# Attention output products scaled and added to the residual by VectorE, in a decoder layer on one core

## Chip, cores and metric

One core of a Trainium2 chip runs the whole layer in one launch. The metric is the device time of an execution in microseconds (us), as the median of several runs.

## What is computed

The reference is one decoder layer on x of 128 sequences x 128 tokens x 256 features, fp32. Cut to what matters here:

```python
x = x + attn(layernorm(x))                    # 16 heads of 16, self-attention
x = x + xattn(layernorm(x), ctx, ctx, mask)   # 16 heads of 16, keys and values from ctx
x = x + ffn(layernorm(x))                     # ternary weights, GELU, layernorm inside

def attn(x):
    ...
    out = einsum('bhqk,bhkd->bhqd', softmax(scores), V).transpose(0, 2, 1, 3).reshape(B, S, D)
    return out @ Wo.T + bo
```

The change touches the last line of each attention: the output product `out @ Wo.T`, and its addition to `x + bo`.

## The kernel before

**Jobs and slots.** The sequences are taken in 32 groups of 4 (G = 4, so 512 tokens). Each group is a self-attention job and, some slots later, a cross-attention job: 64 jobs in a fixed order, six self jobs first (LEAD = 6), then cross and self in turn, then the last six cross jobs. They run through a software pipeline. In slot n, job n+4 is loaded, n+3 has its moments taken, n+2 is normalised (`s.norm`), n+1 is projected to queries and keys (`s.proj`), n has its scores and maxima taken and its values projected (`s.max`), n-1 its exponentials and weighted sums (`s.exp`), and n-2 its output product and residual (`s.out`). Slots run from -3 to 65. Jobs alternate between two sets of buffers and semaphores, `even` and `odd`; in each slot `a` is the chain of jobs n and n-2, `b` that of n-1 and n+1. After the attention slots comes the feed-forward stage, whose order the change leaves alone.

**Order.** Nothing is scheduled automatically. Each engine's queue in a slot is the list of calls at the end of `pool_slot`, `act_slot`, `dve_slot` and `pe_slot` (SyncE's is in `sp_slot`); engines wait for one another by semaphores.

**Precision.** Products are fp16 in three parts (high x high, low x high, high x low). ScalarE makes the high part by a copy to fp16, GpSimd the low part by subtracting it (`low`, L735). Weights carry a factor WS = 8, so the output product is divided by 8 when it leaves its banks.

**Banks.** TensorE's results lie in four tensors of two banks each: `score_bank` (scores, L1049, with mask matmuls L1030), `exp_bank` (shifted scores, L1067; for cross jobs also the masked values' products, L1167), `out_bank` (weighted sums, L1082) and `product_bank`. The last is shared by three users in turn within a slot: the query and key tiles (L1106), the output products (`products`, L1113, two calls for batches 0, 1 and 2, 3) and the value products (`values`, also L1113). The values may overwrite the banks only when the output products have been read.

**Around the change.** The output product leaves in two steps. ScalarE's `products_out` (L844 to 852) waits for the products (`op_mm`) and for `xs_lo`, as GpSimd must have read the normalised values from `xn` before `xn` is written; it copies both banks, scaled by 1/WS, to `xn` and raises `op_out`. GpSimd's `residual` (L749 to 752) then adds the block `xb` (input plus output bias, made by `biased` at L764 two slots earlier) and raises `y_ready`, on which SyncE's `store` waits. TensorE's `values` waits for `op_out`:

```python
if s.out:
    pe.wait_ge(a.op_out, s.out.k + 1)
```

**VectorE in a slot.** Eight score maxima (`maximum`, L906, a reduction of 128x1024 out of `score_bank`), four query and key tiles (L912), four quarter outputs (`outputs`: a transposition L940, for cross jobs an addition L947, a reciprocal L951 and a product L955), two transpositions of the attention output (`turn_att`, L961), then the negated maxima (`negate`, L967 or L969) and the moments (L980 to L986). The order of its second half is `maximum(5)`, `outputs(b, s.exp, 1)`, `turn_att(b, s.exp, 0)`, `maximum(6)`, `outputs(b, s.exp, 2)`, `maximum(7)`, `negate()`, `moments()`. TensorE's is `products(2, 3)`, `shifted(6)`, `scores(6)`, `weighted(2)`, `values(0, 1)`, `scores(7)`, `shifted(7)`, `values(2, 3)`, `turn_maxima()` (L1148, waits for `negate`), `masked_values()` (L1167, waits for ScalarE's `values_out`, L857), `weighted(3)`. ScalarE's is `exps(5)` (L811), `products_out()`, `exps(6)`, `exps(7)`, `values_out`.

Of the kernel before, what the change touches and what calls it, by code (L numbers as in the profile page):

```python
# [12 lines left out]
ALU = mybir.AluOpType  # L13
# [499 lines left out]
class Chain:  # L513
# [3 lines left out]
    def __init__(self, name, sb, sem):  # L517
# [49 lines left out]
        self.op_mm = sem(n + "_op_mm")  # L567
        self.op_out = sem(n + "_op_out")
        self.y_ready = sem(n + "_y_ready")


def attention(nc, program, ins, sh, x1_dram, x2_dram, prep):
# [19 lines left out]
    with ExitStack() as stack:  # L592
# [137 lines left out]
        def pool_slot(pool, s, bias_done=None):  # L730
# [17 lines left out]

            def residual():  # L749
                if s.out:  # L750
                    pool.wait_ge(a.op_out, s.out.k + 1)
                    nc.gpsimd.tensor_tensor(xn[:, :, :], xn[:, :, :], a.xb[:, s.out.k % 2], ALU.add).then_inc(a.y_ready, 1)

            def biased():
# [26 lines left out]
            low_norm()  # L781
            residual()
            biased()
# [4 lines left out]
        def act_slot(s):  # L788
# [3 lines left out]
            def await_store():  # L792
                if s.past:
                    act.wait_ge(stored_by(s.past), 16 * (s.past.g + 1))
# [48 lines left out]

            def products_out():  # L844
                if s.out:
                    act.wait_ge(a.op_mm, s.out.k + 1)
                    if s.norm:
                        act.wait_ge(a.xs_lo, s.norm.k + 1)
                    else:
                        await_store()  # L850
                    act.activation(xn[:, :, :].rearrange("p b d -> p (b d)"), pbank[:, :, :].rearrange("p a d -> p (a d)"),
                                   ACT.Copy, scale=1.0 / WS).then_inc(a.op_out, 1)

            def values_out(n):
# [31 lines left out]
            exps(5)  # L886
            products_out()
            exps(6)
# [8 lines left out]
        def dve_slot(s):  # L897
# [59 lines left out]
            def turn_att(ch, job, kt):  # L957
                if job:

                    dve.wait_ge(ch.ao_ready, 4 * job.k + 2 * kt + 2)  # L960
                    dve.transpose(attT[:, kt], att[:, kt]).then_inc(ch.aT_ready, 1)  # L961

            def negate():
                if s.max:
# [43 lines left out]
            outputs(b, s.exp, 1)  # L1008
            turn_att(b, s.exp, 0)
            maximum(6)  # L1010
            outputs(b, s.exp, 2)
# [10 lines left out]
        def pe_slot(s):  # L1022
# [106 lines left out]
            def values(*batches):  # L1129
                if s.max is None:  # L1130
                    return
                for g in batches:
                    if g == 0:
                        if s.out:
                            pe.wait_ge(a.op_out, s.out.k + 1)
                        elif s.proj:
                            pe.wait_ge(b.qk_lo, 4 * s.proj.k + 4)
# [371 lines left out]
```

## Time and profile before

| | |
|---|---|
| median of 3 runs | 2367.21 us (2365.73 to 2368.36) |
| profiled execution, its own time | 2370.91 us |
| its span, first to last instruction | 2369.1 us |
| mean granted TensorE clock | 0.984 of full speed |
| two neighbouring slots in the middle | 25.17 and 26.85 us |

The profile is of one execution. Times in timelines are from the start of the span. The attention slots end at about 1796 us, the rest is the feed-forward stage. PE is TensorE's matmuls, PEld its weight loads, DVE VectorE, ACT ScalarE, POOL GpSimd, SP SyncE; L906 is line 906 of the kernel. In a timeline a bracket names the idle time of the engine ahead of the row and what ended it; a row without one began with no idle time worth naming. Matmul rows overlap by some hundredths of a us, since matmuls are pipelined.

### The profile page before, as it was taken

To read this page: it belongs to the slowest core of one execution; us is meant where nothing else is said; L and a number is where in the kernel's file an instruction comes from. 1 tells how busy PE (TensorE), PEld (TensorE's weight loads), DVE (VectorE), ACT (ScalarE), POOL (GpSimd) and SP (SyncE) were. 2 spreads that over 40 slices of the span, in tenths; PEclk is the share of its full clock that TensorE was granted. 3 is DMA by queue.
4 is the path that set the end of the run, shared out by engine and by line. 5 is a ranking of instruction groups with operands and counts; after the bars stand their busy time and mean duration, and the time that the engine had idled before them with its cause. 6 is when DMAs were issued, how large, how long until landed. Compare 5 with 4: busy or idle time off the path is not lost.

```text
span 2369.1 us, 70234 instructions
## 1 busy us (share of the span) xinstructions
PE 2183.7 (92%) x29033; PEld 1449.4 (61%) x29033; DVE 1933.5 (82%) x3903; ACT 1596.8 (67%) x2354; POOL 1044.4 (44%) x849
## 2 busy tenths in 40 slices
PE   4689999999999999999999999999967999999999
PEld 2356656656665666566566656655544777777776
DVE  5788888888888888888888888887745788887887
ACT  3377666667666666666666666665535878778786
POOL 2144443454444344444434444454224554555543
PEclk9799999999999999999999999999978999999999
DMA  4567666676666667666666766676422333333332
GB/s 129 117 151 175 156 144 155 145 158 157 157 153 152 155 140 159 157 160 153 154 150 143 153 161 157 159 173 144 89 59 54 84 103 80 97 89 83 103 81 63
DMA packets 472860, 311.01 MB, mean 131 GB/s; under 512 B 288144, under 2 KB 423184, under 8 KB 472592
## 3 DMA queue, kind: packets, MB, share of 16 engines
q1 hardware_dynamic: 469488, 306.80, 55.0%
q8 instruction: 205, 3.36, 0.6%
q10 hardware_dynamic: 3104, 0.34, 0.1%
q14 instruction: 63, 0.52, 0.1%
HBM read 71.65 MB, written 50.33 MB: 51 GB/s over the span
## 4 chain that ended last, share of the span: by engine, by line
PE 65%; DVE 18%; ACT 7%; issue 7%; SPq 1%; DMA 1%; POOL 1%; DVEq 0%; ACTq 0%; POOLq 0%
PE product_bank L1106 14%; PE ybk L1434 9%; PE hbk L1458 9%; PE out_bank L1082 7%; PE tbk L1448 5%; ACT prob L811 4%; PE product_bank L1113 4%; PE score_bank L1030 4%; DVE out_bank L940 4%; PE score_bank L1049 3%; DVE odd_mx L906 3%; PE exp_bank L1067 3%; PE exp_bank L1030 3%; PE exp_bank L1167 3%; DVE att L955 2%
## 5 line engine op out<-in xcount | busy, mean ns | idle before, releaser
L811 ACT ACTIVATE prob<-exp_bank 128x1024 f32<-128x1024 f32 x512 | 523.1, 1022 | 254.6 <-PE exp_bank L1067 246.6
L735 POOL TENSOR_TENSOR xs<-xn,xs 128x1024 f16<-128x1024 f32 x64 | 136.3, 2130 | 638.8 <-ACT xs L835 638.8
L906 DVE TENSOR_REDUCE even_mx<-score_bank 128x8 f32<-128x1024 f32 x256 | 310.5, 1213 | 97.4 <-PE score_bank L1049 97.4
L906 DVE TENSOR_REDUCE odd_mx<-score_bank 128x8 f32<-128x1024 f32 x256 | 310.2, 1212 | 81.0 <-PE score_bank L1049 81.0
L801 ACT ACTIVATE qk<-product_bank,bcol 128x512 f16<-128x512 f32 x256 | 175.9, 687 | 232.0 <-PE product_bank L1106 228.7
L1458 PE MATMUL hbk<-wfcT,ffn_xhl 128*128 128x512 f16 x1024 | 264.5, 382 | 6.3 <-ACT hid L1355 3.4
L1418 DVE SCALAR_TENSOR_TENSOR ghl<-tbk,lnwc,ghl 128x512 f16<-128x512 f32 x256 | 188.0, 735 | 100.3 <-ACT ghl L1349 100.3
L1434 PE MATMUL ybk<-wpT,ghl 128*128 128x256 f16 x2048 | 260.5, 273 | 0.8 <-DVE ffn_y L1403 0.7
L1434 PEld LDWEIGHTS ybk<-wpT,ghl 128*128 128x128 f16 x2048 | 197.8, 98 | 66.1 <-DVE ghl L1418 0.9
L1349 ACT ACTIVATE ghl<-tbk,lnwc 128x512 f16<-128x512 f32 x256 | 174.1, 681 | 68.1 <-PE tbk L1448 68.1
L940 DVE STREAM_TRANSPOSE out_bank<-out_bank 128x512 f32<-128x512 f32 x256 | 183.5, 717 | 24.8 <-PE out_bank L1082 24.7
L912 DVE SCALAR_TENSOR_TENSOR qk<-product_bank,bcol,qk 128x512 f16<-128x512 f32 x256 | 184.2, 740 | 22.4 <-ACT qk L801 22.4
L1030 PE MATMUL exp_bank<-maskBT,pick 64*128 64x512 bf16 x1024 | 156.5, 385 | 45.3 <-ACT prob L811 27.7
L1113 PE MATMUL product_bank<-WT,ahl 128*128 128x256 f16 x1536 | 192.9, 276 | 4.8 <-POOL ahl L735 4.8
L735 POOL TENSOR_TENSOR ahl<-attT,ahl 128x512 f16<-128x512 f32 x128 | 148.6, 1161 | 100.6 <-ACT ahl L816 100.6
L1379 DVE BATCH_NORM_STATS2 hstats<-hid 128x6 f32<-128x512 f32 x256 | 174.1, 680 | 16.5 <-ACT hid L1355 16.4
L1355 ACT ACTIVATE hid<-hbk 128x512 f32<-128x512 f32 x256 | 152.4, 596 | 51.0 <-PE hbk L1458 44.0
L1106 PE MATMUL product_bank<-odd_xhl,WT 128*128 128x512 f16 x732 | 176.0, 384 | 7.6 <-DVE qk L912 5.6
L1113 PEld LDWEIGHTS product_bank<-WT,ahl 128*128 128x128 f16 x1536 | 141.4, 99 | 34.3 <-POOL ahl L735 5.1
L1030 PE MATMUL score_bank<-maskB,pick 64*128 64x512 bf16 x1024 | 154.7, 381 | 6.3 <-DVE even_mx L906 5.6
L1448 PE MATMUL tbk<-ident,hid 128*128 128x128 f32 x1024 | 154.4, 274 | 0.7 <-ACT hid L1355 0.7
L1458 PEld LDWEIGHTS hbk<-wfcT,ffn_xhl 128*128 128x128 f16 x1024 | 98.2, 98 | 75.1 <-ACT hid L1355 5.2
(174 smaller groups left out, 4401.3 us busy)
## 6 DMA issues: line engine op xcount, KB each, us to landing
even_stk<-qk SPq DMA_DIRECT2D x384, 128.0 KB, 2.7
odd_stk<-qk SPq DMA_DIRECT2D x384, 128.0 KB, 2.8
x_scratch<-xn SPq DMA_DIRECT2D x64, 512.0 KB, 4.8
ctx_in<-in_ctx SPq DMA_DIRECT2D x32, 512.0 KB, 4.6
ffn_src<-x_scratch SPq DMA_DIRECT2D x32, 512.0 KB, 3.8
out<-ffn_y SPq DMA_DIRECT2D x32, 512.0 KB, 3.7
odd_src<-in_x SPq DMA_DIRECT2D x29, 512.0 KB, 5.4
even_src<-x_scratch SPq DMA_DIRECT2D x29, 512.0 KB, 5.5
```

The source lines that it names most:

```text
L735: nc.gpsimd.tensor_tensor(out, src, hi, ALU.subtract).then_inc(lo_ready, 1)
L811: act.activation(prob[:, p % 3], ebank[:, :, :], ACT.Exp, scale=EXP_SCALE).then_inc(b.exp_done, 1)
L906: dve.tensor_reduce(a.mx[:, g * H:(g + 1) * H].rearrange("p (r e j) -> p r e j", r=2, e=2)[:, :, eight], sbank[:, :, :].rearrange("p r (j ...
L912: dve.scalar_tensor_tensor(qk[:, 3 * (n // 2), n % 2], pbank[:, n % 2], sh.bcol[:, 2 * s.proj.which + n // 2, n % 2:n % 2 + 1], qk[:, 1 + ...
L940: dve.transpose(obank[:, 1], obank[:, 0]).then_inc(ch.o_turned, 1)
L1030: pe.matmul(bank[:, r].rearrange("p (b s) -> p b s", b=G), sh.pick[rows, h], mask[rows, h].unsqueeze(1).broadcast_to([HALF, G, S]), start= ...
L1106: last = pe.matmul(pbank[:, n % 2].rearrange("p (b s) -> p b s", b=G), sh.WT[:, (s.proj.wq, s.proj.wk)[n // 2], wp, kt, n % 2 * P:(n % 2 + ...
L1113: last = pe.matmul(pbank[:, g // 2, g % 2 * D:(g % 2 + 1) * D], stationary(part, g, kt), sh.WT[:, w, wp, kt, :], start=(k == 0 and kt == 0 ...
L1418: dve.scalar_tensor_tensor(ghl[:, LO, s], tbk[:, TURN_BANK[s]], sh.lnwc[:, s:s + 1], ghl[:, HI, s], ALU.mult, ALU.subtract).then_inc(glo_r ...
L1434: last = pe.matmul(ybk[:, b], ghl[:, part, t, b * S:(b + 1) * S], sh.wpT[:, t], start=(t == 0 and part == HI and b % 2 == 0), stop=(t == F ...
L1448: last = pe.transpose(tbk[:, TURN_BANK[s], b * S:(b + 1) * S], hid[:, 1 - half, b, s * P:(s + 1) * P], sh.ident[:, :])
L1458: last = pe.matmul(hbk[:, s % 2], xhl[:, half, part, s // 2, kt], sh.wfcT[:, kt, s % 2 * HF:(s % 2 + 1) * HF], start=(part == HI and kt == ...
```

## The change

ScalarE's `products_out` and GpSimd's `residual` go, and with them the semaphore `op_out`. VectorE gets a `residual` that reads both banks, multiplies by 1/WS, adds `xb` and writes `xn`, in one operation; it stands between `turn_att(b, s.exp, 0)` and `maximum(6)`. TensorE's value products wait for `y_ready`, which this operation raises.

```diff
@@ pool_slot
-            def residual():
-                if s.out:
-                    pool.wait_ge(a.op_out, s.out.k + 1)
-                    nc.gpsimd.tensor_tensor(xn[:, :, :], xn[:, :, :], a.xb[:, s.out.k % 2], ALU.add).then_inc(a.y_ready, 1)
...
             low_norm()
-            residual()
             biased()
@@ act_slot
-            def products_out():
-                if s.out:
-                    act.wait_ge(a.op_mm, s.out.k + 1)
-                    if s.norm:
-                        act.wait_ge(a.xs_lo, s.norm.k + 1)
-                    else:
-                        await_store()
-                    act.activation(xn[:, :, :].rearrange("p b d -> p (b d)"), pbank[:, :, :].rearrange("p a d -> p (a d)"),
-                                   ACT.Copy, scale=1.0 / WS).then_inc(a.op_out, 1)
...
             exps(5)
-            products_out()
             exps(6)
@@ dve_slot
+            def residual():
+                if s.out:
+                    dve.wait_ge(a.op_mm, s.out.k + 1)
+                    dve.wait_ge(a.xb_ready, s.out.k + 1)
+                    if s.norm:
+                        dve.wait_ge(a.xs_lo, s.norm.k + 1)
+                    elif s.past:
+                        dve.wait_ge(stored_by(s.past), 16 * (s.past.g + 1))
+                    dve.scalar_tensor_tensor(xn[:, :, :].rearrange("p b d -> p (b d)"), pbank[:, :, :].rearrange("p a d -> p (a d)"), 1.0 / WS,
+                                             a.xb[:, s.out.k % 2].rearrange("p b d -> p (b d)"), ALU.mult, ALU.add).then_inc(a.y_ready, 1)
...
             turn_att(b, s.exp, 0)
+            residual()
             maximum(6)
@@ pe_slot, values
                         if s.out:
-                            pe.wait_ge(a.op_out, s.out.k + 1)
+                            pe.wait_ge(a.y_ready, s.out.k + 1)
```

**VectorE's queue**, second half of a slot whose newest job is a self job (odd chain) and whose exponentials are of a cross job. Rows are line, operation, output<-inputs, the semaphores waited for. Before:

```order
L955 TENSOR_TENSOR att<-out_bank,rec 128x16x16 [waits even_rec_ready]
L961 STREAM_TRANSPOSE attT<-att 128x512 [waits even_ao_ready]
L906 TENSOR_REDUCE odd_mx<-score_bank 128x2x4 [waits odd_s_mm]
L940 STREAM_TRANSPOSE out_bank<-out_bank 128x512 [waits even_pv_done,even_ao_ready]
L947 TENSOR_TENSOR out_bank<-out_bank,ue 128x16x17 [waits even_o_turned]
```

And with the change:

```order
L937 TENSOR_TENSOR att<-out_bank,rec 128x16x16 [waits even_rec_ready]
L943 STREAM_TRANSPOSE attT<-att 128x512 [waits even_ao_ready]
L953 SCALAR_TENSOR_TENSOR xn<-product_bank,odd_xb 128x1024 [waits odd_xs_lo,odd_xb_ready,odd_op_mm]
L888 TENSOR_REDUCE odd_mx<-score_bank 128x2x4 [waits odd_s_mm]
L922 STREAM_TRANSPOSE out_bank<-out_bank 128x512 [waits even_pv_done,even_ao_ready]
```

One operation has come in ahead of maximum 6, with three waits; the order is otherwise the same.

**TensorE's queue** at the value products of an early slot. Before:

```order
L1082 MATMUL out_bank<-prob,odd_vals 32x128 [waits odd_o_turned,odd_exp_done]
L1082 MATMUL out_bank<-prob,odd_vals 32x128 x15
L1113 MATMUL product_bank<-WT,even_xhl 128x256 [waits even_op_out]
L1113 MATMUL product_bank<-WT,even_xhl 128x256 x11
L1049 MATMUL score_bank<-even_stk 128x128 [waits even_max_done]
```

And with the change:

```order
L1076 MATMUL out_bank<-prob,odd_vals 32x128 [waits odd_o_turned,odd_exp_done]
L1076 MATMUL out_bank<-prob,odd_vals 32x128 x15
L1107 MATMUL product_bank<-WT,even_xhl 128x256 [waits even_y_ready]
L1107 MATMUL product_bank<-WT,even_xhl 128x256 x11
L1043 MATMUL score_bank<-even_stk 128x128 [waits even_max_done]
```

Nothing has moved on TensorE; one wait has another semaphore, raised by another engine.

## Rows read from the trace of the kernel before

**Rows 1.** The page: busy time by engine, and the chain that ended last.

```profile
PE 2183.7 (92%) x29033; PEld 1449.4 (61%) x29033; DVE 1933.5 (82%) x3903; ACT 1596.8 (67%) x2354; POOL 1044.4 (44%) x849
...
PE 65%; DVE 18%; ACT 7%; issue 7%; SPq 1%; DMA 1%; POOL 1%; DVEq 0%; ACTq 0%; POOLq 0%
```

**Rows 2.** Lines L851 and L752: durations min/median/max in ns; waiters in us and times.

```profile
L851 ACT ACTIVATE xn<-product_bank x64: 1024/1026/1030, 139.8 to 1794.6; 128x1024 f32<-128x1024 f32 x64
...
  PEld product_bank L1113: 3.2, 5
  PE product_bank L1113: 1.9, 4
...
L752 POOL TENSOR_TENSOR xn<-xn,even_xb x32: 2353/2356/2373, 140.9 to 1780.5; 128x1024 f32<-128x1024 f32 x32
```

**Rows 3.** Two neighbouring slots: length, then busy us of PE, PEld, DVE, ACT, POOL.

```profile
814.38:839.55 25.17, 23.59 (x367) 15.05 (x366) 21.83 (x35) 17.15 (x23) 8.28 (x8) 1.00 0.58 134
839.55:866.40 26.85, 25.71 (x413) 16.58 (x414) 23.09 (x46) 18.35 (x26) 15.00 (x13) 1.00 0.75 172
```

**Rows 4.** VectorE by line, whole span: count | busy us, mean ns | idle before.

```profile
L906 DVE TENSOR_REDUCE even_mx<-score_bank 128x8 f32<-128x1024 f32 x256 | 310.5, 1213 | 97.4 <-PE score_bank L1049 97.4
...
L912 DVE SCALAR_TENSOR_TENSOR qk<-product_bank,bcol,qk 128x512 f16<-128x512 f32 x256 | 184.2, 740 | 22.4 <-ACT qk L801 22.4
...
L1403 DVE SCALAR_TENSOR_TENSOR ffn_y<-ybk,hrstd,ffn_y 128x256 f32<-128x256 f32 x128 | 52.8, 474 | 1.1 <-PE ybk L1434 1.1
```

**Rows 5.** Timeline, second half of a C slot: start us, us, engine, line.

```profile
803.37 2.13 POOL L735 TENSOR_TENSOR xs<-xn,xs 128x1024 f16<-128x1024 f32 x1 [8.69 <-ACT xs L835]
...
803.48 1.49 PE L1113 MATMUL product_bank<-WT,ahl 128*128 128x256 f16 x12
...
806.65 1.19 DVE L906 TENSOR_REDUCE even_mx<-score_bank 128x8 f32<-128x1024 f32 x1
...
806.89 1.48 PE L1113 MATMUL product_bank<-WT,ctx_hl 128*128 128x256 f16 x12
...
807.76 0.71 DVE L940 STREAM_TRANSPOSE out_bank<-out_bank 128x512 f32<-128x512 f32 x1
...
809.46 1.02 ACT L811 ACTIVATE prob<-exp_bank 128x1024 f32<-128x1024 f32 x1 [1.94 <-PE exp_bank L1067]
...
811.52 1.99 PE L1167 MATMUL exp_bank<-even_vals,maskcT 128*32 128x256 f32 x32 [0.22 <-ACT even_vals L857]
```

**Rows 6.** Timeline, second half of the S slot that follows.

```profile
833.79 1.19 DVE L906 TENSOR_REDUCE odd_mx<-score_bank 128x8 f32<-128x1024 f32 x1
...
833.98 1.48 PE L1113 MATMUL product_bank<-WT,odd_xhl 128*128 128x256 f16 x12
...
838.01 0.23 DVE L969 TENSOR_TENSOR odd_negm<-odd_mx,mshift 128x64 f16<-128x64 f32 x1
...
838.29 0.33 PE L1148 MATMUL score_bank<-ident,odd_negm 128*16 128x128 f16 x3 [0.42 <-DVE odd_negm L969]
```

**Rows 7.** Timeline of VectorE, start of slot 4.

```profile
171.42 0.75 DVE L912 SCALAR_TENSOR_TENSOR qk<-product_bank,bcol,qk 128x512 f16<-128x512 f32 x1 [0.64 <-ACT qk L801]
```

**Rows 8.** Timeline, a slot of the last six (cross jobs alone).

```profile
1615.76 1.18 DVE L906 TENSOR_REDUCE odd_mx<-score_bank 128x8 f32<-128x1024 f32 x1
...
1616.38 0.83 PE L1113 MATMUL product_bank<-WT,ctx_hl 128*128 128x256 f16 x6
```

**Rows 9.** Timeline, end of attention, slot 65.

```profile
1794.63 1.02 ACT L851 ACTIVATE xn<-product_bank 128x1024 f32<-128x1024 f32 x1 [6.62 <-PE product_bank L1113]
...
1795.73 2.34 POOL L752 TENSOR_TENSOR xn<-xn,odd_xb 128x1024 f32<-128x1024 f32 x1 [6.49 <-ACT xn L851]
```

**Rows 10.** Timeline of TensorE, two waits for VectorE at about 1630 and 1661.

```profile
1629.60 1.47 PE L1106 MATMUL product_bank<-ctx_hl,WT 128*128 128x512 f16 x6 [1.84 <-DVE qk L912]
...
1661.28 2.25 PE L1106 MATMUL product_bank<-ctx_hl,WT 128*128 128x512 f16 x6 [1.83 <-DVE qk L912]
```

**Rows 11.** The stretch after the second: columns as in rows 3, then clock, DMA, GB/s.

```profile
1661.00:1666.00 5.00, 4.72 (x32) 1.97 (x33) 2.77 (x5) 2.29 (x3) 1.16 (x1) 0.66 0.47 89
```

More of the change, by code:

```diff
@@ L567, in __init__ @@
         self.op_mm = sem(n + "_op_mm")
-        self.op_out = sem(n + "_op_out")
         self.y_ready = sem(n + "_y_ready")
```

## Prediction, made blind

> **What bounds the kernel now.** I read the page first, then the chain that ended last, then the timelines of two neighbouring slots, since shares of busy time say little about which wait ends last. The page [rows 1] shows TensorE busy for 92% of the span, VectorE 82%, ScalarE 67% and GpSimd 44%. So the change takes work from the two engines with room and gives it to one that has little. The chain of waits [rows 1] runs 65% over TensorE, 18% over VectorE, 7% over ScalarE and 1% over GpSimd. The reader should see that GpSimd's additions are practically never on it.
>
> The two removed instructions are 64 ScalarE copies of 1.03 us and 64 GpSimd additions of 2.36 us [rows 2]. Who waited for them? Nobody for the additions. The copies held TensorE 5 times in its weight load, 3.2 us in all, and 4 times in its matmul, 1.9 us in all [rows 2]; the store of the block of rows stands on SyncE's queue behind the transfer of the maxima, which comes later in the slot anyway. About 5 us is therefore all that the whole removal can give back inside the slots.
>
> A slot is one pass of the pipeline; the two kinds in the middle take 25.17 and 26.85 us [rows 3]. From its middle on, VectorE alternates between score maxima and the quarter outputs, and TensorE alternates between scores, shifted scores, weighted sums and products. Call a slot **C** when its newest job is cross-attention (slots 6, 8 to 58) and **S** when it is self-attention with a cross job in the exponentials (7, 9 to 57). These are 27 and 26 slots; 2 to 5 are self alone, 59 to 63 cross alone, 64 and 65 the tail.
>
> **The new instruction.** A VectorE operation on 128x1024, fp32 from the banks, fp32 from SBUF and to SBUF, does not occur before. The same operation on 128x256 takes 474 ns, one on 128x512 (fp16 out) 740 ns, and a reduction that reads 128x1024 out of a bank 1213 ns [rows 4]. From 256 to 512 elements the price is 266 ns, 1.04 ns per element. So 1024 elements cost 740 + 512 x 1.04 = 1273 ns. Ends: 1.21 us (the reduction, the nearest in size) and 1.48 us (twice the 512 one, its fixed part paid twice). I take 1.27 us. On VectorE the following instruction starts some 0.08 us before the end of the one in front (the maximum of 806.65 lasts 1.19 us, its successor starts at 807.76 [rows 5]), so the queue is moved by 1.27 - 0.08 = **1.19 us**.
>
> **S slots.** The operation stands behind the transposition of the outputs and ahead of maximum 6. What it waits for is there by then, as the C slot below shows with its numbers. It starts where maximum 6 started, at 833.79 [rows 6]. From there to the negation at 838.01 no row of VectorE carries idle time, and TensorE starts the transposition of the maxima behind it at 838.29 [rows 6]; the last weighted sum and the next slot's projections stand behind that. This is the place where VectorE is the bound: +1.19 us. TensorE's own new wait costs no more: the value products now wait for y_ready, which comes at 833.79 + 1.27 + 0.06 = 835.12 where they started at 833.98 [rows 6], 1.14 us, in parallel. 26 x 1.19 = **30.9 us**.
>
> **C slots.** Here VectorE starts maximum 6 at 806.65 [rows 5]. The products (12 matmuls from 803.48, 1.49 us) are ready at 804.97 and GpSimd's low part at 803.37 + 2.13 = 805.50 [rows 5], so again only VectorE's queue sets the start. y_ready comes at 806.65 + 1.27 + 0.06 = 807.98; the value products started at 806.89 [rows 5]. TensorE waits 1.09 us. Queued behind them on TensorE are scores 7 and shifted scores 7, for which ScalarE waits with its last exponential at 809.46; then come ScalarE's values, the masked products at 811.52 [rows 5] and the next slot. VectorE's negation, also 1.19 us later, stays just hidden beside this. 27 x 1.09 = **29.4 us**.
>
> **The rest.** In slots 2 to 5 VectorE is the bound as in S: 4 x 1.19, of which one slot gives back 0.64 us, since VectorE waits there for ScalarE, and that for the stacking transfers [rows 7]: 4.1 us. In 59 to 63 TensorE has more work: maximum 6 starts at 1615.76, so y_ready is at 1617.09 where the products started at 1616.38 [rows 8]: 5 x 0.71 = 3.6 us. In slot 65 the copy starts at 1794.63 and the addition ends at 1795.73 + 2.34 = 1798.07 [rows 9]; the next stage's first variance stands behind it on GpSimd. The new operation would end at 1794.63 + 1.27 = 1795.90, 2.2 us sooner, but the aggregation of the means now stands behind it on VectorE, and the GELU, which has its own table load and matmuls ahead, takes over soon: I count -1 us. Removed ScalarE time otherwise comes at a point where it next waits for TensorE: nothing.
>
> Sum: 30.9 + 29.4 + 4.1 + 3.6 - 1.0 = **+67 us**. The profiled execution took 2370.9 us (span 2369.1), the median of the runs is 2367.2: 3.7 us lower. I set the forecast on the median: 2367.2 + 67 = 2434, and give **2435 us**.
>
> **Two rules weighed.** The rows first: VectorE without idle time in the second half of S, 82% over the span [rows 1, 6]. The Trainium skill, page Perfetto Trace Analysis, section Optimizing Scalar/DVE Operations, says that a saturated VectorE is a reason to hand work to ScalarE or even GpSimd; this change does the reverse. By that rule alone every slot would pay the full step, 64 x 1.19 = 76 us, against 67 by the rows.
> The other speaks for the change: GPSIMD Engine Reference, section Engine selection, sends elementwise additions to VectorE, as GpSimd needs about twice the time for two inputs. The trace agrees on the durations (2.36 against an expected 1.27 us [rows 2, 4]), but nobody waits for the 2.36.
>
> **The rivals.**
> - *The released engines were the bound* (the other side, faster). ScalarE waits for GpSimd's low parts ahead of each copy; without copy and wait its exponential 6 comes over 1 us sooner. For it: 9 waits of TensorE on the copy [rows 2] and the tail [rows 9]. If VectorE's added step hid in its idle time, 5.1 + 1.0 us come back: 2361 us. It decides if y_ready comes before TensorE asks for it, so if VectorE reached the place over 1 us sooner than it does. Against it: VectorE has no gap between the last quarter output and maximum 6 in either slot. Were every copy and addition in series on the path, as the rule on GpSimd would suggest, it would be 64 x (1.03 + 2.36 - 1.27) = 136 us less, 2231 us; that nobody waits for the additions [rows 2] denies it. Both together 0.03.
> - *Only VectorE's own bound counts*. In C slots TensorE's wait is absorbed by the ones it has further on (0.2 us before the masked products [rows 5], others after). Then the 29.4 us fall away: 2405 us. Against it: those waits are for ScalarE, whose work hangs on the same delayed matmuls. 0.07.
> - *The clock falls*. TensorE stands at 2.4 GHz nearly throughout, but from 1661 to 1666 the granted clock was 0.66 [rows 11], partly at 1.2 GHz: six matmuls took 2.25 us after a wait of 1.83, where they took 1.47 after one of 1.84 [rows 10]. The stretch lost 5 x 0.34 = 1.7 us. The new waits are near 1.1 us each, and each slot goes on as densely as before. If they did bring it in each C and S slot, it would be 53 x 1.7 = 90 us more: 2525 us. 0.05. The Trainium skill (TensorE: Matmul & The Clock Gate, Part 1) says that idleness sends the clock back to its lower level; by rows 10 a single wait of 1.8 us may or may not do it.
> - *Nothing measurable*, because both new waits are covered by something that I don't see: 0.02.
>
> **The numbers.** My forecast has 0.83. Its own bounds: with 1.21 us for the operation 58 slots give 3 to 4 us less; with 1.48 us, 12 us more. Two more waits on the instruction (three semaphores instead of one) are not priced by any row: between nothing and 0.1 us each, 12 us more. If a part of the C slots' wait is absorbed (half: 15 us less), it is about 2417. Range **2410 to 2460**; outside lie the 2405 case, the clock case and the fast ones, under 2 in 10. Within 0.2% is 4.7 us, about what a measurement of this kernel can tell from no change. Faster 0.03, same 0.02, slower 0.95.
>
> **What would show it.** VectorE has 64 operations of about 1.27 us from product_bank to xn, without a wait ahead of them in slots 2 to 63, and its busy time is 81 us higher; ScalarE's is 66 us lower, GpSimd's 151 us. TensorE has a new wait at the value products on VectorE, about 1.1 us and 58 times. C and S slots are each 1.1 to 1.2 us longer, a pair 54.3 instead of 52.0 us, and the stage behind attention keeps its length. I am wrong if the operation takes over 1.5 us, if slots grow by less than half of this while the wait is there (absorption), if the granted clock falls in the middle of attention, or if VectorE reaches the place with idle time ahead.

## The result, and the profile after

| | before | with the change |
|---|---|---|
| median of the runs | 2367.78 us (4 runs, 2365.73 to 2368.45) | 2435.15 us (4 runs, 2433.18 to 2435.99) |
| profiled execution, its own time | 2370.91 us | 2435.99 us |
| its span | 2369.1 us | 2434.2 us |

The ratio is 1.0279, with a 95% interval from 1.0264 to 1.0294: the change makes the kernel 2.8% slower, 67 us. The forecast was 2435 us.

The page of the changed kernel, the lines of [rows 1]:

```profile
PE 2190.0 (90%) x29033; PEld 1450.1 (60%) x29033; DVE 2004.9 (82%) x3967; ACT 1537.4 (63%) x2290; POOL 892.7 (37%) x785
...
PE 60%; DVE 22%; issue 9%; ACT 6%; DMA 1%; SPq 0%; POOL 0%; DVEq 0%; ACTq 0%; POOLq 0%
```

ScalarE has become 59 us less busy, GpSimd 152 us less, VectorE 71 us more. The 64 removed ScalarE copies lasted 66 us; the remaining ScalarE operations count some 6 us more than before. In the chain that ended last VectorE's share rose from 18% to 22% and TensorE's fell from 65% to 60%, while GpSimd's went from 1% to nothing. Over 200 us of work left two engines, and the kernel became longer: neither was what the slots waited for.

The new operation, by its line, with those who waited for it:

```profile
L953 DVE SCALAR_TENSOR_TENSOR xn<-product_bank,even_xb x32: 1183/1185/1186, 143.1 to 1848.4; 128x1024 f32<-128x1024 f32 x32
L953 DVE SCALAR_TENSOR_TENSOR xn<-product_bank,odd_xb x32: 1183/1184/1224, 167.3 to 1862.7; 128x1024 f32<-128x1024 f32 x32
its engine sat idle before it (us, times) until:
  PE product_bank L1107: 7.0, 1
who waited for it (us, times):
  PEld product_bank L1107: 75.4, 62
  PE product_bank L1107: 58.9, 62
```

It takes 1.18 us, a little less than foreseen, and VectorE stood idle ahead of it once, in the tail. TensorE's matmuls waited for it in each of the 62 slots that have value products, 58.9 us in all: 0.95 us each. ScalarE's copy had held them 4 times, 1.9 us in all [rows 2]. The weight load in front of the matmuls waits for the same event, so its own sum (75.4 us now, 3.2 us before) is not added to theirs.

Two neighbouring slots, each from the first projection matmul to the next slot's, S and then C. The columns are those of [rows 3]:

```profile
845.57:871.87 26.30, 23.66 (x367) 15.06 (x365) 22.95 (x36) 16.16 (x22) 6.00 (x8) 1.00 0.55 128
871.87:899.71 27.84, 25.77 (x415) 16.56 (x413) 24.07 (x48) 17.50 (x25) 12.54 (x11) 1.00 0.73 166
```

Against 25.17 and 26.85 us [rows 3] they are 1.13 and 0.99 us longer. TensorE does the same 23.7 and 25.8 us of work at the same full clock; the added time is idle time on it.

The timeline of a C slot, the place of [rows 5]:

```profile
835.82 0.42 DVE L937 TENSOR_TENSOR att<-out_bank,rec 128x256 f32<-128x256 f32 x1
...
836.27 0.71 DVE L943 STREAM_TRANSPOSE attT<-att 128x512 f32<-128x512 f32 x1
836.91 1.19 DVE L953 SCALAR_TENSOR_TENSOR xn<-product_bank,even_xb 128x1024 f32<-128x1024 f32 x1
838.02 1.21 DVE L888 TENSOR_REDUCE even_mx<-score_bank 128x8 f32<-128x1024 f32 x1
...
838.15 1.48 PE L1107 MATMUL product_bank<-WT,ctx_hl 128*128 128x256 f16 x12 [0.93 <-DVE xn L953]
...
840.72 1.02 ACT L804 ACTIVATE prob<-exp_bank 128x1024 f32<-128x1024 f32 x1 [4.10 <-PE exp_bank L1061]
...
841.78 0.28 DVE L960 SCALAR_TENSOR_TENSOR even_negm<-even_mx,mfloor,mshift 128x64 f16<-128x64 f32 x1
...
842.12 0.39 PE L1142 MATMUL score_bank<-ident,even_negm 128*16 128x128 f16 x4
```

And of an S slot, the place of [rows 6]:

```profile
865.05 1.19 DVE L953 SCALAR_TENSOR_TENSOR xn<-product_bank,odd_xb 128x1024 f32<-128x1024 f32 x1
866.16 1.21 DVE L888 TENSOR_REDUCE odd_mx<-score_bank 128x8 f32<-128x1024 f32 x1
...
870.40 0.23 DVE L962 TENSOR_TENSOR odd_negm<-odd_mx,mshift 128x64 f16<-128x64 f32 x1
```

VectorE goes from the transposition (836.27) to the residual to the maximum without a gap, each of the two starting some hundredths before the one in front has ended (836.91 + 1.19 = 838.10, next start 838.02). From the residual's start to the maximum's is 1.11 us, the step by which the queue is moved. ScalarE shows where the freed time went: its last exponential has 4.10 us of idle time ahead, where 1.94 us stood before [rows 5]. TensorE turns the maxima at 842.12 without idle time ahead, though VectorE's negation has moved too: beside TensorE's own wait of 0.93 us that delay stays hidden, as the prediction had it.

The negations of the maxima stand at the same place in each slot, and so cut the span into comparable stretches. From the rows of their two lines, self and cross:

```profile
L962 DVE TENSOR_TENSOR odd_negm<-odd_mx,mshift x29: 225/226/226, 123.7 to 1628.8; 128x64 f16<-128x64 f32 x29
...
L960 DVE SCALAR_TENSOR_TENSOR odd_negm<-odd_mx,mfloor,mshift x3: 283/286/286, 1684.7 to 1814.6; 128x64 f16<-128x64 f32 x3
```

Before, the same rows ran from 120.8 to 1566.1 us (slots 1 and 57) and to 1744.4 us (slot 63).

| stretch | before | after | difference | forecast |
|---|---|---|---|---|
| start to negation of slot 1 | 120.8 | 123.7 | +2.9 | 0 |
| slot 1 to slot 57 | 1445.3 | 1505.1 | +59.8 | 4.1 + 26 x 2.28 = +63.4 |
| slot 57 to slot 63 | 178.3 | 185.8 | +7.5 | 1.1 + 3.6 = +4.7 |
| slot 63 to the end | 624.7 | 619.6 | -5.1 | -1.0 |

A pair of slots grew from 52.00 to 54.16 us, as a mean over slots 6 to 57; the forecast was 54.3.

### The profile page after: what moved, and what is told of

It is laid out like the page before. It is cut to its first block, busy times and chain, and to the rows that moved or that the text cites. A ratio compares the mean times of both kernels' runs of the same rounds, so it can differ in the third digit from the quotient of the medians.

```text
span 2434.2 us, 70170 instructions
## 1 busy us (share of the span) xinstructions
PE 2190.0 (90%) x29033; PEld 1450.1 (60%) x29033; DVE 2004.9 (82%) x3967; ACT 1537.4 (63%) x2290; POOL 892.7 (37%) x785
## 4 chain that ended last, share of the span: by engine, by line
PE 60%; DVE 22%; issue 9%; ACT 6%; DMA 1%; SPq 0%; POOL 0%; DVEq 0%; ACTq 0%; POOLq 0%
PE product_bank L1100 14%; PE ybk L1428 9%; PE hbk L1452 9%; PE out_bank L1076 5%; PE tbk L1442 5%; DVE out_bank L922 5%; DVE odd_mx L888 4%; ACT prob L804 4%; PE score_bank L1024 4%; PE score_bank L1043 3%; PE product_bank L1107 3%; DVE att L937 3%; PE exp_bank L1024 3%; PE exp_bank L1161 2%; PE exp_bank L1061 2%
## 5 line engine op out<-in xcount | busy, mean ns | idle before, releaser
L758 POOL TENSOR_TENSOR even_xb<-even_src,boB 128x1024 f32<-128x1024 f32 x32 | 75.8, 2369 | 224.1 <-DVE even_negm L960 181.4
```

## The experiments

Two theories were put against each other. **Queue**: VectorE is the bound in both kinds of slot or nearly so, and the time is the length of the new operation on its queue. **Wait**: in C slots, and perhaps in all, the time comes from TensorE's value products, which now wait for a later event. Every kernel below ran beside the kernel before on the same chip, for 3 rounds or more, and the ratios are against that. "Pair" is the mean length of two neighbouring slots, 52.00 us before and 54.16 us with the change. S and C slots apart, from the first projection matmul of one slot to that of the next, medians of the profiled execution in us (differences in the text are taken before rounding):

| kernel | S slot | C slot |
|---|---|---|
| before | 25.16 | 26.84 |
| with the change | 26.30 | 27.83 |
| e1_extra_vector | 26.29 | 27.54 |
| e3_residual_sooner | 26.16 | 27.42 |
| e4_busy_released | 26.30 | 27.84 |
| e5_half_residual | 25.77 | 27.30 |
| e8_swap_and_tail | 25.09 | 26.84 |
| e9_weighted_ahead | 24.69 | 27.05 |

### e1_extra_vector: VectorE's time alone

To the kernel before, an operation of the same size is added at the same place. Nothing waits for it, and ScalarE's copy, GpSimd's addition and `op_out` stay.

```diff
+            def extra():
+                if s.out and s.max:
+                    dve.wait_ge(a.xb_ready, s.out.k + 1)
+                    dve.tensor_reduce(scratch[:, :], a.xb[:, s.out.k % 2].rearrange("p b (j k) -> p (b j) k", j=2), AX.X, ALU.max)
...
             turn_att(b, s.exp, 0)
+            extra()
             maximum(6)
```

> The kernel before, with one more VectorE operation of about the length of the new one (a reduction of 128x1024) at the place of the new residual in slots 2 to 63; ScalarE's copy, GpSimd's addition and TensorE's wait for op_out stay, and nobody waits for the extra operation. Theory V (VectorE's queue carries the cost, the wait for y_ready only runs beside it): S and early slots pay the step of about 1.1 us; in C slots scores 7 now wait for maximum 6 and the transposition of the maxima for the negation, 0.9 us; in the last ones 0.6: 26 x 1.1 + 4 + 27 x 0.9 + 3 = +60 us, about 2427. Theory W (TensorE's wait for y_ready carries it in C slots, VectorE's time being hidden there): only the S and early slots, +33 us, about 2400.

Measured: 2424.89 us, ratio 1.0239 (1.0220 to 1.0257), pair 53.84 us. The operation took 1.18 us, 62 times. An S slot is 1.13 us longer than before and a C slot 0.71; with the change these are 1.14 and 1.00. So in S the queue gives all of it. In C it gives 0.71, and TensorE's wait adds another 0.29. The timeline of the C slot shows both the absence of the new wait and the queue's own effect:

```profile
830.20 1.18 DVE L967 TENSOR_REDUCE scratch<-even_xb 128x8 f32<-128x1024 f32 x1
830.44 1.48 PE L1120 MATMUL product_bank<-WT,ctx_hl 128*128 128x256 f16 x12
...
832.57 0.61 PE L1037 MATMUL score_bank<-maskB,pick 64*128 64x512 bf16 x4 [0.64 <-DVE even_mx L907]
...
835.40 0.39 PE L1155 MATMUL score_bank<-ident,even_negm 128*16 128x128 f16 x4 [0.37 <-DVE even_negm L973]
```

The value products start without idle time; scores 7 then wait 0.64 us for maximum 6 and the turned maxima 0.37 us for the negation. The prediction called VectorE's delay in C "just hidden" beside TensorE's wait. With both there, as in the changed kernel, it is (the row at 842.12). But it is hidden by little: where TensorE's wait is absent, as here, VectorE a good microsecond later decides by itself in C as well. GpSimd's additions are still made in this kernel, and its S slots are as long as with the change to 0.01 us, so GpSimd's release gave nothing back there either.

### e2_wait_only: TensorE's wait alone

The kernel before, but the value products wait until GpSimd has added, not until ScalarE has copied.

```diff
-                            pe.wait_ge(a.op_out, s.out.k + 1)
+                            pe.wait_ge(a.y_ready, s.out.k + 1)
```

> The kernel before with one edit: the value products wait for y_ready (GpSimd's addition) instead of op_out. VectorE has no more work. By the rows before, the addition ends at 809.05 in the C slot where the products started at 806.89, and at 836.08 in the S slot where they started at 833.98: TensorE waits 2.2 us in both. If such a wait goes to the end in full: C 27 x 2.2, S 26 x 1.7 (VectorE's lead of 0.4 us over the maxima's transposition is used up first), early 4 x 1.7, last 5 x 1.6: +118 us, about 2485. If most of a wait on TensorE is absorbed by later waits (rival), less than half of that, under 2425.

Measured: 2549.52 us, ratio 1.0764 (1.0745 to 1.0783), pair 57.92 us: 180 us more than before where 118 were expected. TensorE's list of waits:

```profile
PE product_bank L1113 <- POOL xn L752: 130.5, 62, 2.9
```

The mean wait is 2.1 us and the longest 2.9. The waits are not absorbed; the time is even larger than their sum. Part of the excess is the clock. The stretch in the middle of attention, in the kernel before:

```profile
300.00:1600.00 1300.00, 1232.12 (x19398) 790.36 (x19398) 1122.23 (x2000) 889.13 (x1202) 585.95 (x477) 1.00 0.67 154
```

With the change:

```profile
300.00:1600.00 1300.00, 1186.38 (x18627) 758.92 (x18626) 1129.95 (x1969) 807.91 (x1105) 444.90 (x408) 1.00 0.64 147
```

And in e2_wait_only:

```profile
300.00:1700.00 1400.00, 1241.61 (x18716) 786.31 (x18713) 1093.20 (x1929) 853.38 (x1156) 563.05 (x458) 0.96 0.60 138
```

Behind such a wait, of 2.08 us, twelve value matmuls took 2.07 us instead of their usual 1.48:

```profile
916.44 2.07 PE L1113 MATMUL product_bank<-WT,odd_xhl 128*128 128x256 f16 x12 [2.08 <-POOL xn L752]
```

The columns of the stretches are those of [rows 11]; the third number from the end is the granted clock: 1.00 before, 1.00 with the change, 0.96 here. 1.00 is 2.4 GHz throughout; an estimate is that 0.96 means some 8% of the time at 1.2 GHz and the rest at 2.4. A second estimate from these rows: 4% of a pair of 58 us is 2.3 us, and with the 3.8 us per pair that 118 us over 62 slots make it is 6.1, against 5.9 measured.

### e3_residual_sooner: the same operation one place ahead

```diff
-            turn_att(b, s.exp, 0)
             residual()
+            turn_att(b, s.exp, 0)
             maximum(6)
```

> The changed kernel with the residual ahead of the transposition turn_att instead of behind it: y_ready comes 0.57 to 0.64 us sooner, VectorE's queue is as long as before and maximum 6 starts at the same time. Theory V: S slots unchanged, in C slots the transposition of the maxima and scores 7 become the bound, 0.1 to 0.2 us less per C slot: 3 to 6 us less than the changed kernel, about 2430. Theory W: 27 x 0.6 = 16 us less, about 2418.

Measured: 2416.33 us, ratio 1.0202 (1.0183 to 1.0220), pair 53.62 us. This is 19 us less than the change, more than either theory gave. The timeline of the C slot:

```profile
826.76 1.21 DVE L953 SCALAR_TENSOR_TENSOR xn<-product_bank,even_xb 128x1024 f32<-128x1024 f32 x1
827.89 0.70 DVE L943 STREAM_TRANSPOSE attT<-att 128x512 f32<-128x512 f32 x1
828.03 1.49 PE L1107 MATMUL product_bank<-WT,ctx_hl 128*128 128x256 f16 x12 [0.21 <-DVE xn L953]
...
832.59 0.39 PE L1142 MATMUL score_bank<-ident,even_negm 128*16 128x128 f16 x4 [0.37 <-DVE even_negm L960]
```

TensorE's wait at the value products shrinks from 0.93 to 0.21 us and the C slot by 0.41 us: this is the 0.29 us of the wait, and 0.12 us that S gets as well (0.14), though S was expected to stay as it is. The latter belongs to VectorE's queue. With the change `turn_att` comes directly behind the product whose result it turns, and starts 0.03 us after that has ended (835.82 + 0.42 = 836.24, start 836.27); here the residual stands between the two, and `turn_att` starts 0.08 us before the residual has ended (826.76 + 1.21 = 827.97, start 827.89). That makes about 0.1 us per slot, read from the rows. e8_swap_and_tail below separates the same two operations in the kernel before and gets 0.07 us in S slots. Between the spans of the two profiled executions, 2434.2 and 2414.0 us, 14.0 of 20.2 us are the 26 pairs at 0.54, 3.4 lie in the last slots, where TensorE's clock also differs between the two (see slots 57 to 63 below), 3.3 in the start-up, which neither kernel changes, and the last stretch is 0.5 longer. The 14.0 us alone are near the 16 us of theory Wait; but the wait gave only 26 x 0.29 = 7.5 us of them, and the rest is the closed gap.

### e4_busy_released: the released ScalarE time filled again

The change, and ScalarE makes a copy of the same size at the old place, with the old waits; `exps(6)` stands behind it. This copy reads from SBUF and not from the banks, takes 1.06 us instead of 1.03 and also waits for the exponentials ahead of it; GpSimd stays released.

```diff
+                    act.wait_ge(a.op_mm, s.out.k + 1)
+                    if s.norm:
+                        act.wait_ge(a.xs_lo, s.norm.k + 1)
...
+                    act.activation(prob[:, 0], prob[:, 2], ACT.Copy, scale=1.0 / WS).then_inc(a.busy_done, 1)
+                    act.wait_ge(a.busy_done, s.out.k + 1)
...
             exps(5)
+            busy()
             exps(6)
```

> The changed kernel with ScalarE's 1 us given other work: a copy of 128x1024 at the place of the old one, with its old waits for the products and for GpSimd's low part, and with exponential 6 behind it; slots 2 to 63. If the released ScalarE time gives nothing back (mine): within 5 us of the changed kernel, 2430 to 2440. If the release had paid for a part of the added VectorE time (rival): slower by the part that it paid, up to 60 us, over 2450.

Measured: 2433.69 us, ratio 1.0276 (1.0257 to 1.0294), pair 54.16 us, the same as the change (1.0279). ScalarE is busy for 1604 us instead of 1537, and the slots keep their length. What ScalarE was relieved of in slots 2 to 63 gave nothing back.

### e5_half_residual: half of the operation

The change, with a residual over the first of the two banks alone. The second half of each output product is left out of the sum.

```diff
-                    dve.scalar_tensor_tensor(xn[:, :, :] ..., pbank[:, :, :] ..., 1.0 / WS,
+                    dve.scalar_tensor_tensor(xn[:, 0:2, :] ..., pbank[:, 0, :], 1.0 / WS,
```

> The changed kernel with a residual of 128x512 instead of 128x1024: it leaves out the second bank (half of the output product and of the sum), and y_ready and all waits stay. It tells whether the cost follows the operation's length. By 475 ns for 256 and 1184 for 1024 elements the operation takes about 0.71 us, its step 0.63. If the cost follows the length (mine): S and early slots 0.6 each, C slots 806.65 + 0.71 + 0.06 - 806.89 = 0.53, the last ones 0.2, the tail -2: 18 + 14 + 1 - 2 = +31 us, about 2400. If the cost were one of waits, semaphores and handing over, whatever the length (rival): near the changed kernel, over 2420.

Its line in the trace:

```profile
L953 DVE SCALAR_TENSOR_TENSOR xn<-product_bank,even_xb x32: 650/652/653, 139.9 to 1813.3; 128x512 f32<-128x512 f32 x32
```

Measured: 2401.41 us against 2370.19 before, ratio 1.0138 (1.0121 to 1.0155), 31 us more, as expected. Against the kernel before, S slots grew by 0.60 and C slots by 0.47 us. The cost goes with the operation's length: 0.53 us less of it, 0.53 us less per slot of either kind than with the change. Two sizes also give its price: 651 ns for 512 elements and 1184 for 1024, so 1.04 ns per element and 118 ns fixed.

### e6_residual_later: the same operation one place behind

```diff
             turn_att(b, s.exp, 0)
-            residual()
             maximum(6)
+            residual()
```

> The changed kernel with the residual behind maximum 6: VectorE's queue is as long, y_ready comes 1.1 us later. Where only VectorE's time mattered, nothing would change: about 2435. If TensorE's wait comes through in full, it is 2.1 us in C slots (807.76 + 1.18 + 0.05 against 806.89) and 2.15 less the 0.42 us of lead in S slots: 27 x 2.1 + 30 x 1.7 + 5 x 1.8 - 2 = +115 us, about 2483. If waits of over 2 us bring TensorE's clock down as they did where GpSimd raised y_ready, up to 2540.

Measured: 2547.14 us, ratio 1.0753 (1.0735 to 1.0771), pair 58.12 us. TensorE's wait for it and the middle stretch:

```profile
PE product_bank L1107 <- DVE xn L953: 129.1, 62, 2.5
```

```profile
300.00:1700.00 1400.00, 1242.01 (x18740) 786.30 (x18732) 1149.23 (x1976) 809.32 (x1108) 448.11 (x409) 0.96 0.60 138
```

Another engine raises the event than in e2_wait_only and VectorE does the same work as with the change, but TensorE's wait is again 2.1 us in the mean, the granted clock again 0.96 and the time within 3 us the same. Without a fall of the clock 2483 us were expected and with one up to 2540; it is 7 us over even that. Both together show that waits of this length come through in full, and that the clock is lower with them.

### e7_tail_only, e8_swap_and_tail, e9_weighted_ahead: looking for a gain

If the removed work stood on the path in the tail alone, VectorE's operation there alone should gain. e7_tail_only is the kernel before, with VectorE's `residual` in slots 64 and 65 only. e8_swap_and_tail also puts `turn_att` behind `maximum(6)`, e9_weighted_ahead on top of this `weighted(3)` ahead of `turn_maxima()` in self slots, so that TensorE has work while it waits for the negation. Each in short:

```diff
 e7
-                if s.out:
+                if s.out and s.max:
                     pool.wait_ge(a.op_out, s.out.k + 1)
...
+                if s.out and not s.max:
...
             turn_att(b, s.exp, 0)
+            residual()
             maximum(6)
 e8
-            turn_att(b, s.exp, 0)
-            residual()
             maximum(6)
+            turn_att(b, s.exp, 0)
+            residual()
 e9
+            if s.max and not s.max.cross:
+                weighted(3)
             turn_maxima()
             masked_values()
+            if not (s.max and not s.max.cross):
+                weighted(3)
```

> The kernel before, with the new VectorE residual only in slots 64 and 65, where no maxima stand behind it; slots 2 to 63 keep ScalarE's copy and GpSimd's addition. If the change is worth something where VectorE has idle time (mine): slot 65 loses the addition ahead of the next stage's first variance, 2.1 us, slot 64 0.3 us: 2 to 2.5 us less than the kernel before, about 2365.5. If the tail's shorter time in the changed kernel came from TensorE's clock alone (rival): no difference.

> As the last one, and with VectorE's transposition turn_att behind maximum 6 instead of ahead of it, in all slots. The transposition waits for the operation just in front of it to have written; with the maximum between, that gap (0.03 us idle instead of 0.08 overlap) goes, as in the run with the residual moved ahead of it, where S slots were 0.13 us shorter. If VectorE is the bound in S and early slots: 30 x 0.11 = 3.3 us less than the run with the tail alone, about 2362. If it isn't: no difference from that run.

> As the last one, and in slots whose newest job is a self job TensorE does the last weighted sum (1.0 us) ahead of the transposition of the maxima, for which it waited 0.42 us on VectorE's negation. The wait is filled: 0.3 us less in each of 26 S and 4 early slots, 9 us less, about 2353, if the maxima's later transfer (0.6 us) is not on the path; if it is, no gain or up to 18 us more.

| kernel | median | ratio | pair |
|---|---|---|---|
| before, same chip, 26 runs | 2369.70 us | | 52.00 |
| e7_tail_only | 2367.53 us | 0.9995 (0.9986 to 1.0004) | 52.00 |
| e8_swap_and_tail | 2368.66 us | 1.0003 (0.9994 to 1.0012) | 51.93 |
| e9_weighted_ahead | 2364.24 us | 0.9979 (0.9969 to 0.9990) | 51.77 |

e7 can't be told from the kernel before by its time, so between its two expectations (2365.5 us or no difference) the medians don't decide; its trace shows the shorter tail (below). The swap shortens each S slot by 0.07 us, where 0.11 were expected, and leaves C slots as they are: 2 us in all, too little to measure. e9 is 0.2% faster than the kernel before, 2364 us where 2353 were expected. Its S slots are 0.40 us shorter than those of e8, more than the 0.3 expected, but the C slots behind them are 0.21 us longer; through what, no run shows. It is the one version that beats both kernels.

### e10_pointer_scale: why the operation was cheaper than priced

The change, with the factor 1/WS read from a column of [128, 1] instead of standing in the instruction. Both rows from which the price was worked out, L912 and L1403 [rows 4], are operations with such a column.

```diff
-                    ... pbank[:, :, :].rearrange("p a d -> p (a d)"), 1.0 / WS,
+                    ... pbank[:, :, :].rearrange("p a d -> p (a d)"), sh.eighth[:, :],
```

> The changed kernel, with the factor 1/WS read from a column of one value per partition instead of from the instruction. The blind price of the operation was 1.27 us, built on two rows whose scalar is such a column (474 ns for 256 elements, 740 for 512: 207 ns beside 1.04 ns per element); measured were 651 ns for 512 and 1184 for 1024, so 118 ns. If the column is what those rows pay for, the operation now takes 1.27 us and 58 slots grow by 0.09 us: 2440 us, 5 more than the changed kernel. If the operands' types or the places make the difference: 1184 ns and no change.

```profile
L955 DVE SCALAR_TENSOR_TENSOR xn<-product_bank,eighth,even_xb x32: 1240/1243/1246, 140.1 to 1849.2; 128x1024 f32<-128x1024 f32 x32
```

Measured: 2436.22 us against 2370.12, ratio 1.0281 (1.0264 to 1.0298), pair 54.28 us. The operation takes 1243 ns, 59 more than with the constant. The blind price was 1273 ns; so 59 of the 89 ns that it was too high are the column. For the rest the place is a candidate: the same instruction with the constant takes 1211 ns in e3_residual_sooner, directly behind the product, and 1208 ns in e6_residual_later, directly behind maximum 6, so 24 to 27 ns more than behind the transposition. The pair follows, 0.12 us longer for twice 0.059.

## Why the prediction held, point by point

**What bounds.** Held. ScalarE's release gave nothing back inside the slots (e4_busy_released), GpSimd's none in S slots (e1_extra_vector keeps its additions), and VectorE had no idle time where the new one stands: the only idle time ahead of it is in the tail. The 5.1 us that the prediction put down as the most that could come back counts one wait twice, for the weight load and for the matmul behind it; the four waits of the matmuls are one each in slots 2 to 5, 1.9 us in all.

**The price of the operation.** Mis-sized: 1.27 us taken, 1.18 measured, and the step on the queue 1.11 us instead of 1.19. It lies below the lower end of 1.21. The slope of 1.04 ns per element was right; the fixed part was 207 ns by the rows with a column, 118 by the operation without. e10_pointer_scale shows two thirds of this; the other 30 ns stay open. The place alone moves the operation by 24 to 27 ns, and the rows also wrote fp16 or read smaller tiles.

**S slots.** Right in kind: 1.14 us measured, 1.13 without TensorE's wait (e1_extra_vector). 1.19 was too much by the price of the operation.

**C slots.** Size nearly right (1.00 against 1.09 us), and so is the path: TensorE's wait is the longer one, and VectorE's own delay is just hidden beside it (the row at 842.12; TensorE's list of waits has none for the negation of a C slot). What the prediction didn't price is how long the hidden path is. e1_extra_vector has 0.71 us without any wait of TensorE's for the new operation. The two don't add up, they are two paths to the same turned maxima; the longer decides, and with the change TensorE's is 0.29 us longer. TensorE waited 0.93 us, not 1.09; 0.09 of this is the shorter operation.

**Slots 57 to 63.** Mis-sized: 7.5 us measured against 4.7. Here TensorE waits at the start of a slot for VectorE's query tiles, 1.84 us before [rows 10]. With a later VectorE this wait is longer. The changed kernel's timeline:

```profile
1694.36 2.21 PE L1100 MATMUL product_bank<-ctx_hl,WT 128*128 128x512 f16 x6 [2.37 <-DVE qk L894]
...
1728.80 2.51 PE L1100 MATMUL product_bank<-ctx_hl,WT 128*128 128x512 f16 x6 [2.34 <-DVE qk L894]
```

Before, one of the two groups of six took 1.47 and one 2.25 us [rows 10]; now both take over 2.2. The term that was mis-sized is "5 x 0.71": it saw the wait at the value products and not what stands queued behind VectorE at the next slot's start. Part of the 2.8 us is scatter of the clock, though. Two groups of e3_residual_sooner and one of e7_tail_only, which in these slots is the kernel before:

```profile
1676.54 1.47 PE L1100 MATMUL product_bank<-ctx_hl,WT 128*128 128x512 f16 x6 [2.62 <-DVE qk L894]
...
1709.21 2.74 PE L1100 MATMUL product_bank<-ctx_hl,WT 128*128 128x512 f16 x6 [2.63 <-DVE qk L894]
```

```profile
1661.55 1.47 PE L1118 MATMUL product_bank<-ctx_hl,WT 128*128 128x512 f16 x6 [1.83 <-DVE qk L912]
```

Behind equal waits the same six matmuls are fast once and slow once, in one execution (e3) as between two (1.83 us here and in [rows 10]). The stretch from slot 57 to 63 accordingly takes 177.1 us in e7_tail_only and 178.3 in the kernel before. How much of the 7.5 us is VectorE and how much the clock stays open.

**The tail.** -1 us foreseen, -5.1 measured from slot 63 to the end. From the last output products to the first variance of the next stage it was 8.7 us before and is 6.6 now. Before:

```profile
1789.29 5.30 PE L1113 MATMUL product_bank<-WT,ahl 128*128 128x256 f16 x24 [4.80 <-POOL ahl L735]
...
1798.03 0.20 POOL L1314 TENSOR_TENSOR ffn_ve<-ffn_mv,eps 128x4 f32<-128x4 f32 x1
```

With the change:

```profile
1857.71 4.97 PE L1107 MATMUL product_bank<-WT,ahl 128*128 128x256 f16 x24 [4.80 <-POOL ahl L734]
...
1862.71 1.22 DVE L953 SCALAR_TENSOR_TENSOR xn<-product_bank,odd_xb 128x1024 f32<-128x1024 f32 x1 [6.95 <-PE product_bank L1107]
...
1864.32 0.20 POOL L1308 TENSOR_TENSOR ffn_ve<-ffn_mv,eps 128x4 f32<-128x4 f32 x1 [6.66 <-DVE ffn_mv L1391]
```

1.8 of these 2.1 us are the removed step: from the start of the copy [rows 9] to the variance it was 3.40 us, from the start of the new operation it is 1.61. The other 0.3 us are the products, 4.97 us instead of 5.30. In e7_tail_only, with the new tail alone, the way from the products to the variance is 6.7 us as well. The remaining 3 us of the 5.1 don't come from the change's tail: e1_extra_vector, whose tail is that of the kernel before, has the stretch from slot 63 to the end 3.1 us shorter. In slot 64 twelve output products took 2.11 us before and take 1.49 now, so TensorE's clock came up sooner; what brings it up sooner stays open.

```profile
1773.14 2.11 PE L1113 MATMUL product_bank<-WT,ahl 128*128 128x256 f16 x12
```

```profile
1842.33 1.49 PE L1107 MATMUL product_bank<-WT,ahl 128*128 128x256 f16 x12
```

**The sum.** 67 us were foreseen and 67 measured on the medians, 65.1 on the two spans. Part of that is luck: by stretches the 26 pairs came out 3.1 us lower than foreseen, slots 2 to 5 0.5 lower, the last slots 2.8 higher, the tail 4.1 lower. The first stretch, 2.9 us longer, is start-up ahead of any changed instruction; in e1, e3 and e5 it is 120.3 to 120.4 us, so this is scatter of the profiled execution.

**The rivals.** *Released engines*: fell by e4_busy_released for ScalarE. GpSimd's time was not filled again in any run; against it stand the S slots of e1_extra_vector and that nobody waited for the additions [rows 2]. *VectorE's own bound alone*: fell in its own form, since nothing of the C slots' wait was absorbed; what remains of it is that 0.71 of the 1.00 us would be there from VectorE's queue alone. *Nothing measurable*: fell with the 67 us. *The clock*: it didn't fall in the middle of attention, 1.00 from 300 to 1600 us, but it was nearer than 0.05 suggests. Waits of about 1 us in each slot left it at 1.00, with waits of 2.1 us it was 0.96. The Trainium skill (TensorE: Matmul & The Clock Gate, Part 1), by which idleness sends the clock back, is borne out by e2 and e6 and not by the change.

**The rules weighed.** That of the Trainium skill's page GPSIMD Engine Reference, section Engine selection, which sends elementwise additions to VectorE, is true of the durations here, 1.18 us for both steps against 1.03 and 2.36 [rows 2], and cost 2.8%. That of the Trainium skill's page Perfetto Trace Analysis, section Optimizing Scalar/DVE Operations, to take work off a saturated VectorE, is the one that the time followed.

## What to carry over

Ask of an operation that is to be moved who waits for it now, and who will; in this kernel the 2.36 us of GpSimd that nobody waited for were cheaper than 1.18 us on the queue that the slot hangs on. Where two engines are nearly in step, price both paths to their next meeting point and take the longer, as either alone gives most of the cost. If the operation must stay on VectorE, put it where its waiter is earliest served and between two operations that depend on each other: one place sooner saved 19 us, one place later cost 112.

## What the runs showed of the hardware

- A VectorE `scalar_tensor_tensor` of 128x1024 in fp32, from the banks and SBUF to SBUF, takes 1184 ns with a constant and 1243 with a column of [128, 1] behind a transposition; with half the elements and a constant, 651 ns. Behind a product or a reduction the one with a constant took 1211 and 1208 ns.
- On VectorE an operation that depends on the one directly ahead starts about 0.03 us after its end; one that doesn't starts 0.08 us before it.
- With waits of TensorE of 0.95 us in each slot of some 27 us the granted clock stayed at 1.00 (2.4 GHz). With waits of 2.1 us at the same place it was 0.96 over 1400 us, so partly 1.2 GHz, and more time was lost than the waits' own sum: 180 us for 130.5 us of waits in e2_wait_only, 177 for 129.1 in e6_residual_later. No wait of TensorE in the first 1300 us of that stretch was longer than 2.13 us.
- A single wait doesn't settle the clock behind it: after 1.83 and 1.84 us, six matmuls of 128x512 took 1.47 us twice and 2.25 us once, after 2.62 and 2.63 us 1.47 and 2.74.
